# A loop body that holds two rounds instead of one

## The reference

```python
x = L0(x, ctx, ctx, ctx, mask, ...)   # chunked attention, 8 heads, chunks of 64, + x, layer norm
x = L1(x, ctx, ...)                   # attention over the channels, 32 heads, LoRA weights, + x
x = L2(x, ctx, ctx, ctx, mask, ...)   # as L0
x = L3(ctx, x, ..., k=30)             # 30 nearest neighbours, small MLP, weighted sum, + x
```

```python
pd = 2.0 * jnp.einsum('bdn,bdm->bnm', p, p) - xx[:, :, None] - xx[:, None, :]
idx = jax.lax.top_k(pd, k)[1]
```

## Time and profile before

| | us |
|---|---|
| median of 3 timed runs | 7017.76 |
| lowest and highest of them | 6999.0, 7027.35 |
| the profiled execution, its own time | 6984.93 |
| its span, from the first to the last instruction | 6983.1 |
| TensorE, matmuls busy | 6195.4 (89% of the span) |
| VectorE busy | 6047.0 (87%) |
| ScalarE busy | 4321.9 (62%) |
| GpSimd busy | 2693.2 (39%) |
| mean granted TensorE clock | 0.95 of full speed |

### The profile page before, as it was taken

The page is one execution under the profiler, slowest core; times in us unless marked ns, Lnnn a source line. Parts: engine busy times, 40 slices in busy tenths (PEclk is TensorE's granted clock), DMA queues, the critical chain, the costliest instruction groups (busy, mean ns, idle before and its releaser), DMA issues.

```text
span 6983.1 us, 208271 instructions
## 1 busy us (share of the span) xinstructions
PE 6195.4 (89%) x79430; PEld 4459.4 (64%) x79430; DVE 6047.0 (87%) x8509; ACT 4321.9 (62%) x10325; POOL 2693.2 (39%) x3399
## 2 busy tenths in 40 slices
PE   8999999999999999999999999999995795888888
PEld 4666666666666666666666666666664234888878
DVE  6999999989999999999999999999996578777776
ACT  4666666666666666666666666666662156666666
POOL 2444444454444444444444454444443101111110
PEclk9999999999999999999999999999997898999999
DMA  3222222222222222222222222222224003222222
GB/s 118 76 75 72 71 71 68 69 75 80 76 72 78 72 68 68 72 75 76 71 72 68 69 72 83 72 75 75 75 70 133 21 16 76 63 64 62 64 66 59
DMA packets 301388, 499.32 MB, mean 72 GB/s; under 512 B 103859, under 2 KB 217699, under 8 KB 299683
## 3 DMA queue, kind: packets, MB, share of 16 engines
q1 hardware_dynamic: 246733, 389.60, 18.3%
q10 hardware_dynamic: 53589, 95.21, 4.3%
HBM read 410.45 MB, written 74.30 MB: 69 GB/s over the span
## 4 chain that ended last, share of the span: by engine, by line
DVE 41%; PE 29%; issue 21%; DMA 5%; ACT 2%; DVEq 1%; SPq 0%; POOL 0%; ACTq 0%; POOLq 0%
DVE pd L1680 10%; DVE m L1670 9%; DVE idx L1676 8%; PE SCA L901 7%; PE PD L1137 6%; DVE mx L1692 4%; PE SCA L1124 3%; DMA gat<-low_scratch 3%; DVE gat L1624 3%; PE SCB L1124 3%; DVE gat L1994 2%; PE SCB L733 2%; PE SCA L1042 1%; PE SCB L1042 1%; PE TP L1050 1%
## 5 line engine op out<-in xcount | busy, mean ns | idle before, releaser
L1670 DVE MAX8 m<-pd 128x8 f32<-128x1024 f32 x1024 | 1244.3, 1220 | 154.5 <-issue 72.1
L1676 DVE FIND_INDEX8 idx<-m,pd 128x8 uint32<-128x1024 f32 x1024 | 1245.2, 1218 | 0.0
L529 POOL TENSOR_TENSOR prod<-prod,hm 128x480 f32<-128x480 f32 x384 | 396.2, 1032 | 1934.8 <-ACT prod L1310 1923.9
L1680 DVE MATCH_REPLACE8 pd<-m,pd 128x1024 f32<-128x1024 f32 x768 | 928.2, 1209 | 0.4
L1192 ACT ACTIVATE pd<-PD,xxcol 128x512 f32<-128x512 f32 x514 | 368.7, 717 | 722.3 <-PE PD L684 692.3
L708 PEld LDWEIGHTS MISC<-ptab,gat 128*128 128x128 bf16 x23400 | 642.3, 96 | 177.7 <-DVE gat L1624 87.7
L1994 DVE TENSOR_TENSOR gat<-maskT,con 120x2048 f32<-120x2048 f32 x256 | 584.0, 2322 | 166.8 <-PE SCA L1124 164.9
L708 PE MATMUL MISC<-ptab,gat 128*128 128x24 bf16 x23400 | 653.2, 174 | 80.8 <-DVE gat L1624 78.3
L1290 ACT ACTIVATE S<-SCA,mx 128x64 f32<-128x64 f32 (+1 forms) x2560 | 590.1, 406 | 118.7 <-DVE mx L1692 118.3
L1290 ACT ACTIVATE S<-SCB,mx 128x64 f32<-128x64 f32 (+1 forms) x2560 | 580.4, 387 | 19.9 <-DVE mx L1692 19.9
L683 PE MATMUL PD<-arena 128*128 128x512 f32 x1028 | 552.6, 619 | 33.0 <-ACT pd L1192 28.3
(11 more groups left out here) (272 smaller groups left out, 14188.3 us busy)
## 6 DMA issues: line engine op xcount, KB each, us to landing
gat<-low_scratch SPq DMA_DIRECT2D x396, 640.0 KB, 3.9
arena<-in_ctx ACTq DMA_DIRECT2D x33, 512.0 KB, 4.2
x_scratch<-arena ACTq DMA_DIRECT2D x33, 512.0 KB, 3.2
x3T_scratch<-reg ACTq DMA_DIRECT2D x33, 512.0 KB, 3.4
maskT<-in_mask SPq DMA_DIRECT2D x32, 512.0 KB
arena<-in_x ACTq DMA_DIRECT2D x32, 512.0 KB, 4.4
reg<-in_ctx ACTq DMA_DIRECT2D x32, 512.0 KB, 3.5
arena<-x3T_scratch SPq DMA_DIRECT2D x32, 512.0 KB, 6.0
```

The source lines that it names most:

```text
L1670: V.max(m, buf[:, :]).then_inc(found, 1)
L1676: last = V.max_index(idx[:, t, 8 * r:8 * r + 8], m, buf[:, :])
L1680: V.match_replace(buf[:, :], m, buf[:, :], -3.0e38).then_inc(found, 1)
```

## The change

On each of the five engines the body of the loop becomes a function `rounds(i)`. A new loop over 16 pairs calls it twice, with `pair * 2` and `pair * 2 + 1`. The order within a round, the waits, the operations and the DMAs are those of before. The body of each loop has twice as many instructions and is run half as often. On GpSimd the counter `steps` is set to 0 in each round; it is a number of the Python program and makes no instruction. The loops of the first and last part are not touched.

```diff
@@ SyncE
-            with sp.Fori(0, NB) as i:
+            def rounds(i):
...
                 spread(i, (i + NB - 1) % NB, (i + NB - 3) % NB)
+
+            with sp.Fori(0, NB // 2) as pair:
+                for u in range(2):
+                    rounds(pair * 2 + u)
@@ GpSimd
-            steps = [0]
-            with pool.Fori(0, NB) as i:
+            def rounds(i):
+
+                steps = [0]
...
+            with pool.Fori(0, NB // 2) as pair:
+                for u in range(2):
+                    rounds(pair * 2 + u)
@@ TensorE
-            with pe.Fori(0, NB) as i:
+            def rounds(i):
...
+            with pe.Fori(0, NB // 2) as pair:
+                for u in range(2):
+                    rounds(pair * 2 + u)
@@ ScalarE
-            with act.Fori(0, NB) as i:
+            def rounds(i):
...
+            with act.Fori(0, NB // 2) as pair:
+                for u in range(2):
+                    rounds(pair * 2 + u)
@@ VectorE
-            with dve.Fori(0, NB) as i:
+            def rounds(i):
...
+            with dve.Fori(0, NB // 2) as pair:
+                for u in range(2):
+                    rounds(pair * 2 + u)
```

## The result

| | before | after |
|---|---|---|
| median of the timed runs, us | 7016.07 (8 runs, 6994.63 to 7035.49) | 6966.99 (8 runs, 6958.69 to 6985.02) |
| profiled execution, us | 6984.93, span 6983.1 | 6977.26, span 6975.5 |
| granted clock, mean of that execution | 0.950 | 0.939 |

The ratio is 0.9937, 95% interval 0.9918 to 0.9956: 49 us faster. The two profiled executions differ by 8 us only. The first experiment took a second profile of before for that reason. So the change in time is read from the timed runs, and the profiles show what happens inside.

A forecast was written before the change was run, and what follows sets the result against it. TensorE's jump stall at each round's end was taken to lie on the path. 2.27 us of stall plus 1.2 of clock make 3.5 us, at 16 inner boundaries 56 us: 7017.76 to 6962, say 6960; range 6915 to 6996.

The forecast's parts named there:

- TensorE starts L733 at once (2.27 us), at the high clock (1.2 us): Inner boundary: L733 follows L684 without the 2.27 us jump stall and runs at 2.4 GHz, worth 1.2 us more.
- the bound of 5.3 us: Inner boundary: ScalarE, free at 402.28, lets scores come at best 5.3 us earlier; 16 times is 85 us, 6933.
- Step 3: ScalarE at the inner boundary: it still needs L733, and its 1.28 us table load behind that wait moves along.
- step 4: VectorE at the inner boundary: it still waits 2.5 us for the scores, so TensorE's gain arrives whole.
- the rival of the low stretches in mid-round: Low clock moves into mid-round, costing 2.4 us every second round; 18 us of gain left, 7000 us; chance 0.10.
- a sign of being wrong: The prediction is wrong if VectorE's mid-round waits grow by what the boundary gives.
- What follows the loop is unchanged: Code behind the loop, 1664 us, only moves address; at most 14 us from 1 us at each of 14 jumps.
- GpSimd's jump: Its 0.2 us jump might become VectorE's 2.9 when doubled; the added 2.7 us is hidden, uncovered 41 us.
- Register arithmetic: 0: Computing `pair * 2 + u` for waits in the loop adds no register instructions, so costs 0.
- The slower rival: Unfolded register arithmetic adds an instruction per wait, 7 us a round uncovered: 168 us more, 7186 us; chance 0.04.
- The step from profile to median: The timed median lay 33 us above the profiled execution; that difference is carried over, giving 6962, say 6960.

The follow-up runs named there:

- The first experiment: The kernel before, unedited, timed against itself for a second profile: 7002.83 us against 7002.49, ratio 1.0005.
- s2: Against before, only TensorE's loop holds two rounds per body; the other four engines jump back every round: 6987.13 us, ratio 0.9972.
- s7: The kernel after, with part of the query products computed twice by TensorE in each round: 6966.58 us, ratio to before 0.9953.
- s8: s4 with the extra columns of s7 and the first queries (L0's) computed twice: 7002.03 us, ratio to before 1.0002.
- s10: The kernel after, with TensorE's aggregation loop placed at slot 0 (instruction number modulo 256): 6995.24 us, ratio to before 0.9980.
- s9: The kernel before, with TensorE's aggregation loop placed at slot 0 (instruction number modulo 256): 7008.45 us, ratio to before 0.9999.
- s11: s7 with TensorE's aggregation loop placed at slot 0 (instruction number modulo 256): 6955.67 us, ratio to before 0.9919.
- s4: The kernel before, one round per body, with the loop's back branch announced on TensorE, ScalarE and VectorE: 6947.76 us, ratio 0.9919.
- s12: s4 with the extra columns of s7, TensorE's aggregation loop placed at slot 0 and its branch announced too: 6890.24 us, ratio to before 0.9832.

## Why the prediction came out right, and where it was wrong

The forecast was 6960 us, measured were 6967, and faster was the likeliest sign. The mechanism is right: the stall behind the jump lay on the path, and it is gone at the 16 inner boundaries. That the number fits so well is luck. The boundary gave more than forecast, the middle of the round took most of it back, and a stage that was priced at nothing added some 16 us.

1. *TensorE starts L733 at once (2.27 us), at the high clock (1.2 us).* Both are shown, at 569.68 and 897.79. The gain that reaches VectorE at an inner boundary was under-sized: its wait before the scores falls to 0.74 us, not to 2.5, because ScalarE's table load left the path as well. VectorE stood idle for 2.33 + 3.69 = 6.0 us and is idle for 0.74 us now: 5.3 us less and not 3.5. That this equals the bound of 5.3 us that I had worked out for ScalarE's chain is chance: that chain still had the table load of 1.28 us, and it left out ScalarE's wait for the keys, 1.26 us at 571.96. Step 3, "moves along", failed in this. The reasoning also had no term for ScalarE's own jump, 2.9 us at each inner boundary of s2 (45.6/16). With all five loops doubled it goes too, and so it took nothing from the sum; but the path needed both jumps gone.

2. *The gain arrives whole (step 4).* It does at the boundary and not at the round's end. The 90 us of the boundaries are met in the two profiles by 74 us of new or larger waits in mid-round (14.2 one-hot DMA, 20.9 distance rows, 16.9 and 5.8 the scores of L823, 8.4 L912's sums, 8.0 VectorE's own chain) and by the 20 us for which VectorE is busy longer. A good part of it is the rival of the low stretches in mid-round, priced at 2.4 us in every second round with a chance of 0.10. It happened in 11 of 15 second rounds, at 3.5 us each (166.8 against 163.3), about 38 us. The other half is not accounted for one by one. I had seen one such round in before (1223.72 to 1389.99) and given it too little weight. The prediction also named, as a sign of being wrong, that VectorE's waits in mid-round grow by what the boundary gives. In the two profiles this sign came nearly whole; that the time fell all the same rests on the timed runs, a third of it on the stage.

3. *What follows the loop is unchanged.* This was the largest error against its size. I allowed 14 us at most, by 1 us for each jump. Against before the stage took 16 us less in after, 25 more in s7 and 77 more in s8. It isn't the jump alone: the body stops in its middle as well, for up to 4.5 us (the lines of s8). Nor is the body "as long" as the main loop's: the records have 2638 instructions in a pass of the stage and 3725 in a round.

4. *GpSimd's jump.* The stall of 2.5 us came as that part of the prediction said, and was hidden as it said. The Trainium skill ("Runtime: NRT & Kernel Launch", Instruction fetch mechanics) has this rule: a taken branch whose target is outside the two blocks held forces a fetch. The trace agrees: 0.2 us with the short body, 2.5 with the doubled one. The size that the page gives for these engines, 512 instructions in two blocks, is no safe bound for a body that jumps back freely: VectorE's body of 393 stalled at each jump all the same (402.0 to 404.9). Whether head and end of that body lay in the two blocks held, no run here shows.

5. *Register arithmetic: 0.* The profile of after bears it out: but for one of 0.4 us, VectorE has no "issue" wait in the loop except at the 15 jumps. The slower rival has nothing in the profile.

6. *The step from profile to median.* I added 33 us to the profiled execution. The result shows why this was necessary: before's profiled execution was quicker than every timed run of it, and that of after one of its slower ones.

Summed up: of the 49 us about 16 are the stage's, an accident of place, and the loop's part is 33 by that subtraction, 16 by s10 against s9, 23 by their profiled loops. Which of these is closest the runs don't settle; all are well below the 56 us forecast for it. Also open is why some pairs lose their gain and others don't. The low clock goes with it, and s7 and s11 show that it can be kept away. Why the clock falls behind the idle 2.2 us before L895 in one round and not in the next I haven't shown. That the place of the stage's body in TensorE's code changes its time is shown by placing it; how the place acts is not, and the time at each slot was only sampled, at six places.

## What to carry to other kernels

Price a jump at the engine that the round's end waits for, and look at every engine that jumps there: halving the jumps of one engine bought next to nothing in the loop, announcing the branches bought more (55 us) than doubling the body (49, of which 16 by accident). Whenever an edit changes the number of instructions ahead of a large loop, compare the time of untouched stages first; if they moved, the total says little about the edit. And a gain at one place of a loop that both engines nearly fill is only kept if the clock holds in the rest of the round, so after such a change look for the low stretches, and for the idle time just before each.

## What the runs showed of the hardware

- A branch announced at the top of the body costs TensorE 0.36 us instead of 3.55 (medians), and VectorE's "issue" wait of 2.33 us disappears. ScalarE's stall stays: 66.0 us in 31 places in s4. In the aggregation stage TensorE's announced branch still costs 2.07 us (s12); why more than in the main loop is not shown.
- The aggregation stage, with the same 2638 instructions of TensorE in each of 15 passes, took from 1117.6 to 1210.3 us with nothing changed but what lies ahead of them and, in s9 to s11, where they are placed. With the branch announced as well it took 1097.9 (s12).
- A body of 285 instructions of GpSimd jumped back in 0.2 us, its double in 2.5; VectorE's of 393 took 2.9 us before and 3.1 doubled (734.5 to 737.6).
- In a doubled body ScalarE's table load at the top of the second round comes 8 us later, just ahead of its first exponentials. The number of loads in the loop stays the same.
- More matmuls can shorten a loop: 16 more of 128 columns in each round (L808: 4608 instead of 4096, 545.2 us and not 488.0) left s11's loop 34 us shorter than s10's. TensorE's busy time in the loop rose by 10 us only (4821.95 to 4831.98), at a mean clock of 0.96 against 0.95.
